# Order of q's stores and gathers on the SP queue of a cross-attention block: high part of the second half first, low part behind the gather for the maxima

## The reference

```python
q = (layer_norm(x) @ q_w).reshape(B, N, 16, 16)
k, v = (layer_norm(context) @ kv_w).reshape(B, M, 2, 16, 16)[:, :, 0], [:, :, 1]
attn = einsum('bnhd,bmhd->bhnm', q, k) * 0.25
attn = softmax(where(xa_mask, -max_float, attn))
x = x + einsum('bhnm,bmhd->bnhd', attn, v).reshape(B, N, C) @ proj_w + proj_b
return x + gelu(layer_norm(x) @ fc1_w + fc1_b) @ fc2_w + fc2_b
```

## Time and profile before

| what | value |
|---|---|
| median of three runs | 800.75 us (799.76 to 800.93) |
| the profiled execution | 797.48 us, span 795.7 us |
| PE, DVE, ACT, POOL busy | 754.7, 625.4, 562.9, 181.0 us |
| one body (288.5 to 334.2 us of the span) | 45.7 us, PE busy 45.2 us |
| q stores, each | 256 KB |
| QR<-qd, two gathers | 480 KB and 96 KB |
| KM<-kd, QM<-qd, three gathers each | 156 KB, 512 KB each |

### The profile page before, as it was taken

One profiled execution on the slowest core, in us unless ns is written; L12 is line 12 of the kernel. 1 busy time (PEld: TensorE's weight loads), 2 busy tenths in 40 slices (PEclk: granted clock), 3 DMA queues, 4 the chain that ended last, 5 costly groups with the idle time before them and its releaser, 6 DMA issues.

```text
span 795.7 us, 16998 instructions
## 1 busy us (share of the span) xinstructions
PE 754.7 (95%) x5615; PEld 636.0 (80%) x5615; DVE 625.4 (79%) x1379; ACT 562.9 (71%) x781; POOL 181.0 (23%) x185
## 2 busy tenths in 40 slices
PE   6748899999999999999999999999999999999998
PEld 6736779788787979788797978879797888878687
DVE  5737788888888888888888798888888888877453
ACT  4618777777867777786767777776777778676732
POOL 3312032222203222220312222030222222031230
PEclk9769999999999999999999999999999999999999
DMA  8777659394775939486684939667593957639100
GB/s 242 151 113 152 93 154 137 117 146 111 150 120 144 130 122 144 104 162 116 146 120 141 134 109 158 127 134 112 151 147 109 142 120 151 116 106 135 32 28 26
DMA packets 89478, 100.47 MB, mean 126 GB/s; under 512 B 9060, under 2 KB 63576, under 8 KB 89432
## 3 DMA queue, kind: packets, MB, share of 16 engines
q1 hardware_dynamic: 88694, 99.55, 65.0%
q10 hardware_dynamic: 754, 0.53, 0.3%
HBM read 69.22 MB, written 30.83 MB: 126 GB/s over the span
## 4 chain that ended last, share of the span: by engine, by line
PE 54%; DMA 17%; DVE 11%; issue 10%; SPq 4%; ACT 2%; POOL 1%; ACTq 0%; DVEq 0%; POOLq 0%
PE A L866 17%; PE F L866 11%; DMA QR<-qd 7%; PE F L990 4%; PE F L992 4%; PE F L991 4%; PE ST L918 4%; DMA kd<-k_lo 3%; DMA qd<-q_lo 3%; DVE g_lo L594 3%; PE ST L936 3%; PE A L945 3%; DVE xT_hi L638 2%; SPq L247 2%; PE A L961 2%
## 5 line engine op out<-in xcount | busy, mean ns | idle before, releaser
L508 ACT ACTIVATE probs<-ST 78x512 f32<-78x512 f32 x256 | 137.7, 588 | 61.2 <-PE ST L936 57.9
L990 PE MATMUL F<-w_hi,g_hi 128*128 128x256 f32 x480 | 138.5, 289 | 0.0
L594 DVE TENSOR_TENSOR g_lo<-g_f,g_hi 128x512 fp32r<-128x512 f32 x128 | 111.1, 868 | 32.9 <-ACT g_hi L542 30.1
L992 PE MATMUL F<-w_hi,g_lo 128*128 128x256 f32 x480 | 133.9, 279 | 0.0
L991 PE MATMUL F<-w_lo,g_hi 128*128 128x256 f32 x480 | 133.8, 279 | 0.0
L528 ACT ACTIVATE QM<-mask_u 77x2048 fp32r<-77x2048 uint8 x64 | 116.9, 1897 | 0.0
L423 POOL TENSOR_TENSOR xin<-xin,projb 128x1024 f32<-128x1024 f32 x16 | 38.2, 2390 | 317.9 <-DMA xin<-in_x 317.9
L936 PE MATMUL ST<-QM,KM 127*78 127x256 f32 x512 | 93.2, 294 | 5.4 <-ACT probs L508 2.2
L990 PEld LDWEIGHTS F<-w_hi,g_hi 128*128 128x128 f32 x480 | 90.3, 188 | 6.2 <-issue 6.2
L991 PEld LDWEIGHTS F<-w_lo,g_hi 128*128 128x128 f32 x480 | 90.5, 189 | 0.0
L936 PEld LDWEIGHTS ST<-QM,KM 127*78 127x78 f32 x512 | 58.9, 146 | 39.6 <-ACT probs L508 25.9
(11 more groups left out here) (168 smaller groups left out, 1859.4 us busy)
## 6 DMA issues: line engine op xcount, KB each, us to landing
QM<-qd SPq DMA_DIRECT2D x48, 512.0 KB, 14.4
xa<-in_x SPq DMA_DIRECT2D x16, 512.0 KB, 3.9
qd<-q_hi SPq DMA_DIRECT2D x32, 256.0 KB, 2.3
qd<-q_lo SPq DMA_DIRECT2D x32, 256.0 KB, 2.3
xin<-in_x SPq DMA_DIRECT2D x16, 512.0 KB, 5.2
QR<-qd SPq DMA_DIRECT2D x16, 480.0 KB, 5.2
out<-xin SPq DMA_DIRECT2D x30, 256.0 KB, 7.3
KM<-kd SPq DMA_DIRECT2D x48, 156.0 KB, 6.8
```

The source lines that it names most:

```text
L508: act.activation(probs[:, quad % NSLOT, 2 * (p % 2):2 * (p % 2) + 2], ST[p % 2][0:MX].rearrange("p (h n) -> p h n", n=N), ACT.Exp, scale=S ...
L594: return dve.tensor_tensor(dst, src, hi.bitcast(F32), ALU.subtract)
L990: pe.matmul(dst, g_hi[:, k, tok], w2_hi[:, k], start=(k == 0), stop=False)
L992: last = pe.matmul(dst, g_lo[:, k, tok], w2_hi[:, k], start=False, stop=(k == HC - 1))
```

## The change

SP stores the high part of q's second half ahead of k's gathers for the maxima; the gather of q for the maxima waits for high stores only; the low store of the second half is issued behind that gather. The low stores count on a semaphore of their own, q_lo_stored, for which the gather of q for the scores, high_o on ACT and q_low on DVE wait.

```diff
-        QM_LOADS, QR_LOADS, K_STORES, Q_STORES = 6 * 16, 6 * 16, 2 * 16, 4 * 16
+        QM_LOADS, QR_LOADS, K_STORES, Q_STORES = 6 * 16, 6 * 16, 2 * 16, G * 16
...
             def store_q(j, g):
-                for part, src, done in ((0, q_hi, q_hi_done), (1, q_lo, q_lo_done)):
-                    sp.wait_ge(done, G * j + g + 1)
-                    sp.dma_start(qd[part, g * P:(g + 1) * P], src[:, g].bitcast(F32)).then_inc(q_stored, 16)
+                store_q_high(j, g)
+                store_q_low(j, g)
+
+            def store_q_high(j, g):
+                sp.wait_ge(q_hi_done, G * j + g + 1)
+                sp.dma_start(qd[0, g * P:(g + 1) * P], q_hi[:, g].bitcast(F32)).then_inc(q_stored, 16)
+
+            def store_q_low(j, g):
+                sp.wait_ge(q_lo_done, G * j + g + 1)
+                sp.dma_start(qd[1, g * P:(g + 1) * P], q_lo[:, g].bitcast(F32)).then_inc(q_lo_stored, 16)
...
             def gather_q_for_scores(j):
                 sp.wait_ge(s_mm, PB * j)
+                sp.wait_ge(q_lo_stored, Q_STORES * (j + 1))
...
                     store_q(j + 1, 0)
+                    store_q_high(j + 1, 1)
                     gather_k_for_maxima(sp, j + 1)
-                    store_q(j + 1, 1)
                     gather_q_for_maxima(j + 1)
+                    store_q_low(j + 1, 1)
                     gather_k_for_scores(sp, j + 1)
...
             def high_o(j, b, nxt):
                 act.wait_ge(q_stored, Q_STORES * nxt)
+                act.wait_ge(q_lo_stored, Q_STORES * nxt)
...
             def q_low(j, g):
                 dve.wait_ge(q_hi_done, G * j + g + 1)
+                dve.wait_ge(q_lo_stored, Q_STORES * j)
```

More of the change, by code:

```diff
@@ L181, in xattn_block @@
         q_stored = sem("q_stored")
+        q_lo_stored = sem("q_lo_stored")
         v_mm = sem("v_mm")
```

## The result

The changed kernel takes 858.22 us, median of four runs (854.69 to 862.41), against 800.84 us before: ratio 1.0705, 95% interval 1.0661 to 1.075. It is slower, as forecast; 842.5 us was predicted, with 820 to 860 as the range. The profiled execution took 862.41 us (span 860.6), the longest of the four.

What follows compares the result with a forecast made beforehand. TensorE, busy 95% of the span, was taken to bound the kernel. A mean loss of 2.58 us in 15 bodies (38.7), plus 3.5, minus 0.4, gave 41.8 us on the 800.75 median: 842.5 us, range 820 to 860.

Steps and rivals of the forecast that it cites:

- The case on which it rested: DMA queue: low store lands with or just behind QR and delays high_o; 842.5 us likeliest, chance 0.78.
- QR's issue at 2.4 us behind q_hi: SP: QR<-qd issued about 2.4 us behind the end of the second q_hi, 1.6 us earlier than before.
- L918's wait gone: PE's maxima matmul: no more waiting for QR<-qd, 9.2 us in 12 of the 16 batch pairs.
- Landing of the low store 6.0 us from QR's first issue: DMA queue: low store lands at 304.38 instead of 299.96, so high_o on ACT starts 4.0 us later.
- high_o to project(0) 2.10 us: ACT, POOL, PE: project(0) follows high_o's start at 304.43 by work and semaphores, at 306.53.
- PE's hole of 2.4 us in the body shown: PE ahead of project(0): stands 2.4 us, as the fc2 groups ahead cover only 1.6 us of the chain.
- project(1) held by the second high_o another 0.5 us: PE: project(1) at 309.85, not 309.34, as the second high_o stands behind QR's mask; 7.7 us in all.
- QR later than that in some bodies: SP: slower KR issues in four bodies send QR out 0.87 us later than reckoned, 3.5 us in all.
- The expected body of 48.4 us: Whole loop body: takes 48.4 us instead of 45.8.
- Rival B: PE's clock falls in the new 2.4 us hole, 1.6 us each, 24 us in all: 867 us; chance 0.05.
- my own case: Low store lands with or just behind QR: 842.5 us likeliest, own range 823 to 856, chance 0.78.
- Rival A: DMA queue: low store overtakes QR or shares the engines, landing at 3.15 us; all holes go: 791 us; chance 0.10.

Runs made afterwards that it cites:

- both repairs: Changed kernel with the low store issued ahead of QR's gather and oT_lo laid over xT_lo, high_o waiting for high stores alone: 794.55 us, ratio 0.9928.

## Why the prediction was right, and where its sizes were off

The case on which it rested, the low store lands with or behind QR's gather and holds high_o, is shown from three sides: the packets run in the queue's order (the store behind KM shows it plainly), moving the store forward or back moves the time by -65 and +62 us, and with the shared bytes gone the same late landing costs nothing.

Step by step. QR's issue at 2.4 us behind q_hi: 2.28. L918's wait gone: gone, but it was PE's wait for 6.5 us in 10 bodies; I had read 9.2 us in 12, which counts the weight loads in as well. Landing of the low store 6.0 us from QR's first issue: 6.2 to 7.1 in the 15 bodies, 6.56 in the mean, so this term was 0.6 us short. In the body shown QR's own packets ran to about 277.5, 4.8 us from the issue, where it was 4.3, and the store's burst and its report came on top of them, not beside them: the last of its packets ran at about 278.4, and it was home at 279.4. high_o to project(0) 2.10 us: 2.12. PE's hole of 2.4 us in the body shown: 2.94 in this one, 3.08 in the mean, so 46 us where 36 stood in the sum. project(1) held by the second high_o another 0.5 us, 7.7 us in all: 0.26 to 0.37 in the four bodies where the clock stayed up, and none in those where it had fallen and project(0) took longer, 1.2 us in all. QR later than that in some bodies, 3.5 us in all: 2.5, in three bodies, and inside the 46. The expected body of 48.4 us is 50.1 in the mean.

Taken together, what PE stands longer is 41.0 us, where the sum had 41.8. That the two agree so well is luck. The holes ahead of project(0), with the late QR in them, came out 7 us longer than the 39.5 forecast and those ahead of project(1) 6.5 us shorter; the old holes gave back 6.5 us where the sum held 4.8.

So what was missing from the 842.5 is the clock, and the step that failed is not a term but a chance. Rival B, the clock falls in the new hole, had 0.05 against one row, the hole of 1.58 us in which it had stayed at 1.00. That row says nothing of a hole of 2.4 us and more. In the changed kernel the clock fell in 11 of 15 bodies. B's price of 24 us is near the deficit in the trace, 25.9 us, but over the time that the clock cost, 15.6 us between medians by the experiment that keeps PE at work. So B came true with a smaller price: without the falls the kernel takes 842.65 us, with them 858.22. That the first is my 842.5 to the tenth is chance, since the landing and the matmuls added are in it too. There is luck in the range as well: 858.22 is above the 856 up to which my own case went, and two of the four runs are above 860.

Rival A, the store overtakes QR, would have given 791. That is what the kernel takes when the store doesn't stand behind QR (792.91), so its price was right and its condition false.

The rule of the Trainium skill that I cited (DMA: Bandwidth & Descriptors, "Queues, rings and completion order") agrees with the trace: in the five kernels that issue the low store behind QR, no landing of it came ahead of QR's packets. That its completion also waits for QR's writes to land is not shown apart; the 0.8 to 0.9 us between the store's last packet and its landing (0.43 in the kernel before) fit it, and fit a slow report as well.

## What to carry to other kernels

A store that looks urgent to nobody can be the release of its source: before moving it back in a queue, list who writes over those bytes next, and price the landing by what stands ahead of it in the queue, not by its own size. Splitting a semaphore so that a consumer waits only for what it reads gave 0.6% here without moving anything; do that first and alone. And a new hole on TensorE can cost more than its length: the matmuls behind it may run at half the clock, so put the hole's own length, and not that of the nearest harmless one, against the rows. A view by line adds up TensorE's matmuls and its weight loads; what the kernel can gain is in the row of the matmuls alone.

## What the runs showed of the hardware

Holes of like length had different ends. In the changed kernel the clock fell behind holes of 2.61, 2.81 and 2.97 us and stayed at 1.00 behind others of 2.55, 2.69, 2.96 and 3.28; with the wait on POOL, holes of 1.9 to 2.4 us left it at 1.00 and those of 2.53, 3.21 and 3.31 brought it down. With the store behind KM all 15 holes, 5.8 to 7.6 us long, did. Even a shorter hole isn't safe: in the first body PE waits 1.7 us for the maxima's result ahead of a transpose (L961 before, L973 after). The kernel before kept its clock there, as did the low store ahead; with oT_lo laid elsewhere, with the count split alone and with both repairs the clock fell, for 1.7 to 3.4 us of deficit.

One fall cost 1.7 us of deficit in eight of the eleven bodies of the changed kernel, 3.4 us in two, and 5.1 us in the first, where it fell twice: windows of 20 us from 76 us on, and of 12 us from 329 and from 380 us on, had a granted clock of 0.74, 0.72 and 0.72.
